# Macaron block on one core: mixer and second feed-forward stage in one program block, first sequence's jobs five to a step

## The reference, cut to what matters

```python
x = hidden_states                                   # 8 sequences x 1024 tokens x 256
x = x + 0.5 * ffn(layernorm(x), w_gate, w_up, w_down)
x = x + mamba(layernorm(x), ...)
x = x + 0.5 * ffn(layernorm(x), w_gate, w_up, w_down)

def ffn(x, ...):                                    # 256 -> 704 -> 256
    gate = q4(x) @ q4(w_gate).T
    up   = q4(x) @ q4(w_up).T                       # q4: fp4 in blocks of 16, quantised and back
    return q4(silu(gate) * up) @ q4(w_down).T

def mamba(h, ...):                                  # 512 channels, 16 states
    x, z = split(layernorm(h) @ in_proj_w)
    x = silu(causal_conv4(x) + conv_b)
    dt, Bm, Cm = split(x @ x_proj_w)                # 64, 16, 16
    delta = softplus(dt @ dt_proj_w + dt_proj_b)
    # along the 1024 tokens: h = exp(delta*A)*h + delta*u*B ;  y = C.h + u*D
    return (y * silu(z)) @ out_proj_w
```

## Time and profile before

| | us |
|---|---|
| three runs: median (lowest to highest) | 3182.69 (3181.71 to 3183.28) |
| the profiled execution, its own time | 3178.54 |
| its span in the trace | 3176.7 |
| PE busy | 2663.4 |
| DVE busy | 2655.6 |
| POOL busy | 2147.2 |
| ACT busy | 1690.8 |

### The profile page before, as it was taken

How to read it: one execution, slowest core, us unless ns; L and a number is a source line. 1 busy time by engine, 2 the same in 40 slices (tenths; PEclk the granted TensorE clock), 3 DMA queues, 4 the chain that set the end, 5 groups by cost and what they waited for, 6 DMA issues and landing times. The chain is left out here.

```text
span 3176.7 us, 31540 instructions
## 1 busy us (share of the span) xinstructions
PE 2663.4 (84%) x10285; PEld 1381.1 (43%) x10285; DVE 2655.6 (84%) x2498; ACT 1690.8 (53%) x2301; POOL 2147.2 (68%) x1283
## 2 busy tenths in 40 slices
PE   3999999957878978978978878878867667999998
PEld 1566556633324414424424424424412123666665
DVE  6788876529999999999999999999999956777775
ACT  3444444436666665666666666666664513444442
POOL 4566654338877877777777787777788734555553
PEclk9999999978979978978978978978976678999999
DMA  3011111028686786777776776776776731111100
GB/s 107 21 50 50 40 56 34 27 68 199 160 201 164 180 193 169 183 178 174 177 188 167 182 191 164 184 179 167 184 178 167 189 79 52 34 34 33 33 27 20
DMA packets 173144, 387.95 MB, mean 122 GB/s; under 512 B 22470, under 2 KB 89990, under 8 KB 172742
## 3 DMA queue, kind: packets, MB, share of 16 engines
q1 hardware_dynamic: 155302, 367.12, 46.4%
q10 hardware_dynamic: 17696, 19.01, 2.0%
HBM read 308.33 MB, written 52.56 MB: 114 GB/s over the span
## 5 line engine op out<-in xcount | busy, mean ns | idle before, releaser
L1229 POOL TENSOR_TENSOR mix_scan<-mix_scan,mix_bc 128x1024 f32<-128x1024 f32 x512 | 1205.2, 2356 | 395.2 <-DVE mix_scan L1310 394.5
L1310 DVE TENSOR_TENSOR_SCAN mix_scan<-mix_decay,mix_ps_du 128x1024 f32<-128x1024 f32 x512 | 1169.9, 2285 | 62.0 <-ACT mix_decay L1267 19.3
L1367 PE MATMUL mix_ps_du<-mix_stack,mix_sel 96*128 96x512 bf16 x1024 | 367.4, 446 | 375.6 <-DVE mix_scan L1310 352.5
L750 PE MATMUL ffn_ps_gate_up<-ffn_w_gate_up,ffn_xT 128*128 128x512 f32 (+1 forms) x1536 | 652.4, 561 | 15.7 <-DVE ffn_h L498 15.5
L1321 DVE TENSOR_TENSOR mix_ps_du<-mix_ps_du,mix_bc 128x1024 f32<-128x1024 f32 x512 | 618.2, 1207 | 48.7 <-PE mix_ps_du L1367 48.2
L1267 ACT ACTIVATE mix_decay<-mix_decay,mix_a_neg 128x1024 f32<-128x1024 f32 x512 | 573.5, 1141 | 109.5 <-DMA mix_decay<-delta_rows 108.7
L750 PEld LDWEIGHTS ffn_ps_gate_up<-ffn_w_gate_up,ffn_xT 128*128 128x128 f32 x1536 | 278.0, 192 | 247.1 <-issue 201.8
L1367 PEld LDWEIGHTS mix_ps_du<-mix_stack,mix_sel 96*128 96x128 bf16 x1024 | 78.7, 103 | 683.0 <-DVE mix_scan L1310 550.3
L1349 PE MATMUL mix_ps_y<-mix_scan,mix_red 128*32 128x512 f32 x2048 | 340.0, 746 | 4.8 <-POOL mix_scan L1229 4.8
L498 DVE TENSOR_TENSOR ffn_h<-ffn_silu_gate,ffn_ps_gate_up 128x704 f32<-128x704 f32 x128 | 113.6, 887 | 272.5 <-ACT ffn_silu_gate L674 268.7
L635 POOL TENSOR_TENSOR ffn_h_scaled<-ffn_h,ffn_h_recip 128x1408 f32<-128x1408 f32 x64 | 168.0, 2625 | 227.7 <-ACT ffn_h_recip L721 227.7
(11 more groups left out here) (167 smaller groups left out, 4103.0 us busy)
## 6 DMA issues: line engine op xcount, KB each, us to landing
mix_decay<-delta_rows SPq DMA_DIRECT2D x512, 512.0 KB, 7.2
mix_stack<-mix_parts SPq DMA_DIRECT2D x384, 64.0 KB, 2.0
delta_rows<-mix_delta SPq DMA_DIRECT2D x32, 512.0 KB, 3.1
ffn_x<-_attn_hidden_states_dram SPq DMA_DIRECT2D x32, 256.0 KB, 3.0
after_ffn<-ffn_y SPq DMA_DIRECT2D x32, 256.0 KB, 3.0
normed_ffn<-ffn_y_normed SPq DMA_DIRECT2D x32, 256.0 KB, 3.2
mix_x_tokens<-normed_ffn SPq DMA_DIRECT2D x32, 256.0 KB, 12.1
mix_x_residual<-after_ffn ACTq DMA_DIRECT2D x32, 256.0 KB, 3.2
```

What stands on the lines that cost most here:

```text
L750: ins = M(psG[:, lo:hi], xT[:, j % 2, (t * KX + k) * P:(t * KX + k + 1) * P], wgu[:, k, lo:hi], start=(k == 0), stop=(k == KX - 1))
L1229: G.tensor_tensor(wt, wt, bc[r % 2][:, 1, :], ALU.mult).then_inc(hc_done, 1)
L1310: V.tensor_tensor_scan(w[:, slot % RING, :], da[:, slot % SPREADS, :], ps_du[:, slot % 2, :], 0.0, ALU.mult, ALU.add).then_inc(scan_done, 1)
L1367: ins = M(ps_du[:, slot % 2, h * 512:(h + 1) * 512], const.sel[0:SEL, i, :], stack[:, c % 2, q, h * 512:(h + 1) * 512], start=True, stop=True)
```

## The change

**First sequence.** The jobs of FIRST_JOBS go five to a step (`PLACES`), in steps 24 to 31. A fifth place is new: place 3, on PE between gate_up(1) and down(1), on ACT behind silu(1); the last place in a step is now 4. `log_delta` stands at k = 36 (step 31, place 1). `add_delta` and `scale_u` stand at the end of POOL's step 31, `leave1` in its step 32, `part3` in its step 33; ACT has `part1` at (32, 4) and `part2` at (33, 1); SP has `keep_delta` in step 33, the first two restacks in steps 34 and 35, and the third behind the last step.

**One block for mixer and second stage.** `ffn` returns five programs, each with a part FIRST (steps up to -1, on DVE up to -2) and REST, and they are called at the end of the mixer's programs. PSUM is one tensor of eight banks (`ps_all`), and both stages take fixed banks of it. The second stage's early tiles (weights, x, xn to xT) lie over mixer tiles that the last sequence does not use; its late tiles (silu_gate to y) over the decay and scan buffers. At slot 48 of the last sequence (`LAST_LOAD_SLOT`) SP issues x of pairs 0 and 1, the weights (1408 and 768 KB) and x of pairs 2 to 5 (256 KB a pair). DVE does its steps -4 to -2 between the last scan and the last gate. The last sequence's four O jobs are carried by the second stage at (-1, 0), (0, 1), (0, 4) and (1, 1); at (2, 0) PE waits for the last of them to be taken, at (7, 0) SP for their stores.

Line numbers move: gate_up is L776 after, the turns L789 to L804, keep_h L687, silu L697, the O matmuls L1122 and L1124, the decay load L1279, B's take L1167, x's load L478, log_delta L1036 and L1038, add_delta L1042, scale_u L1047.

```diff
 def ffn(...)  # sync, step
-            for k in units(j, 0, 1, 2, 3):
+            for k in units(j, 0, 1, 2, 3, 4):
                 ahead.sync(sp, k, sig.yn_stored)
...
 # gpsimd, end of step
+            if ahead is not None:
+                ahead.pool(pool, j)
...
 # scalar, step
             if on(j, i, 0):
                 silu(1, j, i)
+            for k in units(j, 3):
+                ahead.act(act, k)
             if on(j, i, 1):
                 keep_x(1, j, i)
-            for k in units(j, 3):
+            for k in units(j, 4):
                 ahead.act(act, k)
...
 # tensor, step
                 if on(j, i, 0):
                     gate_up(t, j, i, 1)
+                for k in units(j, 3) if t == 1 else []:
+                    ahead.pe(pe, k)
                 if on(j, i, -2):
                     down(t, j, i)
                 if t == 1 and on(j, i, 1):
                     turn_x(1, j, i)
-                for k in units(j, 2 * t + 1):
+                for k in units(j, (1, 4)[t]):
                     ahead.pe(pe, k)
...
-AHEAD = 24
+AHEAD, PLACES = 24, 5
...
+LAST_LOAD_SLOT = 48
...
     def first_sync_end(sy):
-        keep_delta(sy, 0, 0, 0)
-        for s in range(3):
-            restack(sy, 0, 0, s)
+        restack(sy, 0, 0, 2)
...
-        if k == 35:
+        if k == 36:
             log_delta(act, 1)
-
-    def first_act_end(act):
-        part1(act, 1, None)
-        part2(act, 1)
-
-    def first_pool_end(pool):
-        add_delta(pool, 1)
-        scale_u(pool, 0, 0, 0, 1)
-        leave1(pool, 1)
-        part3(pool, 1)
+        if k == 40:
+            part1(act, 1, None)
+        if k == 41:
+            part2(act, 1)
+
+    def first_pool(pool, j):
+        if j == 31:
+            add_delta(pool, 1)
+            scale_u(pool, 0, 0, 0, 1)
+        if j == 32:
+            leave1(pool, 1)
+        if j == 33:
+            part3(pool, 1)
...
+    def last_pe(pe, k):
+        if k < 2:
+            pe.wait_ge(taken["Z"], B * PER_BATCH["Z"])
+        elif k < 4:
+            pe.wait_ge(taken["O"], nth("O", B - 1, k - 2))
+        if k < 4:
+            make(pe, B, B, "O", -1, k, k % 2)
+        if k == 4:
+
+            pe.wait_ge(taken["O"], B * PER_BATCH["O"])
...
 # sync, mixer
+                    if r == B - 1 and slot == LAST_LOAD_SLOT:
+
+                        sy.wait_ge(made["O"], nth("O", B - 2, 3))
+                        for k in range(4):
+                            sy.wait_ge(out_stored[k], 16 * 2)
+                        after.sync(sy, FIRST)
...
 # vector, mixer
+            rounds(dve, program)
+            after.vector(dve, FIRST)
+            gate(B - 1, CHUNKS - 1)
+            after.vector(dve, REST)
...
+    units = {(AHEAD + k // PLACES, k % PLACES): k for k in range(len(FIRST_JOBS))}
+    units.update({(32, 4): 40, (33, 1): 41, (33, 0): 42, (34, 0): 43, (35, 0): 44})
+    first = Carried(units, first_sync, first_sync_end, first_act, first_pool, first_pe)
+    last = Carried({(-1, 0): 0, (0, 1): 1, (0, 4): 2, (1, 1): 3, (2, 0): 4, (7, 0): 5},
+                   last_sync, nothing, last_act, nothing, last_pe)
...
-        mix.run()
-        with ExitStack() as of_ffn2:
-            ps_turned = Alloc(nc, of_ffn2, "ffn2_").ps("turned", [P, 2, 512])
-            block = of_ffn2.enter_context(nc.Block())
...
+        with nc.Block() as block:
+            mix.run(block, two)
```

585 lines of the change are left out of this document (326 added, 259 removed).

## The result

| | before | after | difference |
|---|---|---|---|
| median on the first chip, 4 runs each | 3182.2 (3181.05 to 3183.28) | 3137.94 (3136.93 to 3138.71) | -44.3 |
| profiled executions, span | 3176.7 | 3135.4 | -41.3 |
| median on a second chip, 9 and 4 runs | 3182.96 (3176.71 to 3189.38) | 3140.55 (3139.21 to 3140.94) | -42.4 |

The ratio is 0.9861, 95% interval 0.9844 to 0.9878 (on the second chip 0.9867, 0.9847 to 0.9887): 1.4% faster, 39 to 50 us. The forecast was 3146, 36.7 us of gain.

What follows compares the result with a forecast made beforehand. No engine bounds the whole: PE bounds the second stage, DVE paces the mixer's late slots, nobody is full at the two seams. Savings 12.0 + 24.7 (27.8 - 3.1) = 36.7 us from 3182.69 give 3146; range 3133 to 3164.

Steps and rivals of the forecast that it cites:

- Jobs of the first stage: End of stage 1: seven jobs move ahead into full PE steps, so the last pair's hidden values come 8.7 us later.
- Rival B: Stage 1 gives nothing: each fifth job adds a wait, eight steps cost 10.8 us, total 3157; chance 0.14.
- log_delta and the split: Stage 1's last step: log_delta delays silu 1.3 us, add_delta and scale_u delay the last ffn_hq 3.7 us.
- What follows the last ffn_hq: Stage 1's tail: last down 11.5 us behind (bounds 8.65 to 16), 8.2 to last y, then store landing 3.2 and meeting 0.7.
- The first seam: From stage 1's last gate_up to the mixer's first instruction: 12.0 us saved, bounds 6 to 18.
- Table loads: ACT's table switches: 1.28 us each as traced; the skill's extra 1.38 drain would cost 4.1 more, saving 7.9 instead of 12.0.
- The second seam's start and steps: Mixer's end: first gate_up 8.2 us behind the last gate, step 2 about 43.5 behind it, 27.8 us earlier than before.
- the gaps: Second stage, steps 0 and 1: PE's three waits for DVE's ffn_h, filled by O jobs, save 5.4 us.
- Decay loads: Late mixer: weights and x ahead of ten decay loads, at 235 KB/us, make the mixer 3.1 us late (bounds 0 and 20).
- Rival C: Second stage: full use without a pause lowers TensorE's granted clock; at 0.90 it costs 53 us, giving 3199; chance 0.03.

Runs made afterwards that it cites:

- e2: Changed kernel with only the first stage's change; the second stage in its own block, output jobs at the mixer's end: 3166.61 us.
- e8: Changed kernel with add_delta and scale_u behind the last ffn_hq, the first part behind the taking of the last hidden values: 3133.78 us.
- e10: Changed kernel with the edits of e8 and e6 together: 3130.34 us, ratio 0.9841 to the kernel before.
- e5: Changed kernel with all four last output jobs ahead of the second stage's first gate_up, none in steps 0 and 1: 3150.78 us, one run.
- e6: Changed kernel with ScalarE's taking and store of the first output job moved to the end of step -1: 3136.59 us.
- e7: Changed kernel with two unused 1408 KB DRAM copies behind the weight loads, ahead of the last ten decay loads: 3145.64 us, one run.
- e3: Changed kernel with all first-sequence jobs, log_delta and the split one step earlier, steps 16 to 23 written out: 3134.45 us.
- e11: e10 with the first sequence's first two token loads issued in step 22 instead of 24, steps 16 to 23 written out: 3118.88 us.
- e9: Changed kernel with first-sequence jobs two steps earlier, log_delta, add_delta, scale_u in step 29, leave1 in 30, part3 in 32, plus e6's edit: 3129.77 us.
- e1: Changed kernel with first-sequence jobs four to a step and the split behind the last step, as before; merged block kept: 3154.24 us.
- e4: Changed kernel with add_delta and scale_u behind the last ffn_hq, the first part ahead of the last hidden values' taking: 3139.16 us.

## Why the prediction was right, point by point

**Jobs of the first stage, mis-sized.** 8.7 us were to come ahead of the last gate_up; it ended 6.4 later. B's last job (1.12) stands behind the last gate_up, at the new place 3, and I counted it in front; one ScalarE wait of 0.6 us in the steps before is gone; and this execution had reached step 24 0.6 us earlier. Rival B did not occur: the traces of after and e2 have no wait at place 3.

**log_delta and the split.** Predicted 1.3 + 3.7 = 5.0, measured 20.17 - 14.85 = 5.3. log_delta is 1.1 (e8 and e10, which have only it, are at 15.91), the split 4.3; my 1.3 should have been 1.2 by its own terms (6.56 - 6.08 + 0.7). I had taken 3.7 for the split, between 3.0 and 4.7, because both engines work at once there. They did not: between 660.19 and 666.22 add_delta, VectorE's quantising and scale_u come one after the other, 2.34 + 1.48 + 2.21 = 6.03 us, of which 1.7 were GpSimd's wait before. By the Trainium skill ("Advanced Engine Details and Errata", Mode Summary) GpSimd and the VectorE instructions that use both ports block each other at a shared SBUF port. The trace agrees: 4.3 us are near the 4.7 without any overlap, and 0.28 us of the missing 0.4 are the two hand-overs (1.48 for 1.63, 2.21 for 2.34).

**What follows the last ffn_hq: right by luck.** 11.5 and 8.2 us were predicted, 11.47 and 8.22 measured, and 3.8 to the first load where I had 3.9. Only the 8.2 came about as I had it. I had put the 11.5 between the tail without jobs (8.65) and 16, for the first part and the takings of D and B. The traces of the changed kernel and of e10 show another reason for the 2.8 us above 8.65:

```profile
668.96 0.76 PE L789 MATMUL ps_all<-ident,ffn_hq 128*128 128x128 f32 x5 [4.19 <-POOL ffn_hq L647]
...
670.51 4.63 PE L815 MATMUL ps_all<-ffn_w_down,ffn_hT 128*128 128x256 f32 x10 [0.79 <-ACT ffn_hT L687]
...
674.94 1.27 PE L789 MATMUL ps_all<-ident,ffn_hq 128*128 128x128 f32 x5
```

```profile
665.12 2.43 PE L815 MATMUL ps_all<-ffn_w_down,ffn_hT 128*128 128x256 f32 x10 [0.79 <-ACT ffn_hT L687]
...
667.38 0.71 PE L789 MATMUL ps_all<-ident,ffn_hq 128*128 128x128 f32 x5
```

In the changed kernel TensorE stands still for 4.19 us, because the last ffn_hq is late, and behind that its granted clock is 0.50 from 670.50 to 676.40: the ten matmuls take 2.20 us more and the five transposes 0.56, together 2.8. In e10, where the split does not stand ahead of the last ffn_hq, there is no such wait, the clock is 1.00 from 663.50 to 672.20, and the tail is 8.65 us. So the split ahead of the last ffn_hq cost 4.3 us and 2.8 more through the clock, and the jobs left in the tail cost nothing. e2, e5, e6 and e7, with the same order, repeat it: waits of 3.02 to 4.44 us for ffn_hq and 4.63 us for the ten matmuls behind.

The 3.8 us to the first load matched for another reason, too. I had the last store of y land in 3.2 us. It was issued at about 688.6 and landed 2.5 us later, at about 691.2; SyncE was busy until 691.73 (689.32 + 2.41) with issuing the third restack, which stands behind its last step, and the first load follows at 692.40. The first seam gave 14.1 us where 12.0 were forecast, and the 2.1 more are from the jobs.

**Table loads.** The silu started 0.02 us behind its load's end (648.53 + 1.28, then 649.83). No drain of 1.38 us is seen there.

**The second seam's start and steps.** 8.2 and 43.5 us behind the gate were forecast, 8.70 and 43.30 measured. The first is a sum that came out near with a wrong term: e6 shows that the taking and store of the first output job held the turned x up by 1.9 us. e5 shows that the gaps held the 5.4 us that were booked.

**Decay loads: the term that failed.** I let the 3712 KB go at the rate of the window of decay loads, 235 KB/us, and got 3.1 us of delay. There was none, and 3.8 us were left. From slot 47's exponential to slot 54's are 27.3 us (2505.98 to 2533.26), where I had 33.2. Two windows of the changed kernel, over decay loads alone and over weights and x:

```profile
2506.00:2519.00 13.00, 7.21 (x24) 0.93 (x24) 12.73 (x8) 6.87 (x6) 8.41 (x5) 0.50 1.03 228
2520.00:2531.00 11.00, 7.66 (x26) 1.72 (x26) 10.82 (x7) 0.71 (x1) 7.55 (x4) 0.70 1.06 381
```

The DMA share is full in both, and the rate is 228 GB/s in one and 381 in the other. The six decay loads kept 2.27 us each (226 KB/us). The 13.7 us behind them, less one decay load's 2.3, carried the 3712 KB and two residual loads of 256 KB (landed at 2527.2 and 2528.8): 370 KB/us. A rate read from one kind of transfer was used for another, and a full share was taken for a full rate; e7 shows where the margin ends.

**The end.** Nothing was booked there, and 0.9 us net were lost: 0.8 won in steps 2 and 3, 1.7 lost by the half-speed group. Rival C did not occur: the clock is 1.00.

By the traces: 36.7 forecast, 2.1 more at the first load, 0.3 up to the first scan, 3.1 at the decay loads, 0.9 less at the end: 41.3. The medians' 44.3 on the first chip contain 3 us more, for before's profiled execution was 3.7 under that median and after's 0.7; on the second chip the medians gave 42.4. That the two profiled mixers agree (1871.8 and 1872.0 us) is luck as well: other executions of the same code need up to 10 us more.

## What to carry to other kernels

Price a seam between two blocks by its landmarks (last full instruction, first full instruction) and not by totals: the columns *hq*, *first* and *step 2* repeated to 0.1 us wherever the code was the same, while the whole varied by 10. *down* and *last* did so only where TensorE's clock did: for *down* the same code took 9.83 us in e8 and 8.65 in e10. Before work is carried into the last step of a pipeline, look which engine's queue it stands in and what is behind it: add_delta and scale_u cost 4.3 us ahead of the last ffn_hq and 2.8 more of half clock behind the wait that they caused, nothing behind it, and 6.7 (4.0 of wait, 2.7 of half clock) when the next instruction of their chain stood ahead of a taking. And after a change, read the longest wait that is left on the full engine, even if it is old: one load issued two steps earlier gave 7.7 us, a sixth of what the whole change gave.

## What the hardware showed that I had not expected

- VectorE's quantising of hidden values and GpSimd's instructions take turns: the one that starts first keeps its length, and the record of the other grows by the time it stands. 1.63 became 3.80 us beside add_delta, scale_u 3.61 for 2.34 (after, 660.21 and 662.61), 1.62 became 3.58 beside leave1 (e3). Not every pair does it: in the mixer VectorE's scans (2.29) and GpSimd's products (2.35) overlap and keep their length (after, 2204.74 and 2203.60).
- After a wait of 4.19 us in the last step of stage 1 TensorE's granted clock was 0.50 for 5.9 us (after, 670.50 to 676.40); without the wait it was 1.00 (e10). After a wait of 5.8 us TensorE came back at half the clock, 1.27 us for five transposes in place of 0.71, with a granted clock of 0.70 in the 8 us behind it; in e11, without the wait, the same window has 1.00.
- At the end of the second stage one group of ten matmuls takes 4.1 instead of 2.4 us. In before, e2, e5, e6, e9, e10 and e11 it is off the path, in after (twice), e1, e3, e4, e7 and e8 on it, for 1.7 us: starting the stage's steps 1.9 us earlier (e6) or 3.6 later (e5) behind the gate moved it off, 1.7 later (e7) did not. What triggers it is open.
- On the same DMA engines, decay loads (each row to several partitions) moved 226 KB/us, weights and x together with residual loads 370, a copy within DRAM 345, all at a full DMA share.
